# Starting the early units of the maximum pass at slot 15 instead of slot 17 in a two-layer attention kernel

## The reference

```python
x = x + tanh(g_xattn[0]) * xattn0(layernorm(x), ctx, ctx)   # 16 heads of 8, softmax over 154 keys
x = x + tanh(g_ffn[0])   * ffn0(layernorm(x))               # 4-bit weights, 16-bit quantized activations
x = x + tanh(g_xattn[1]) * xattn1(layernorm(x), ctx, ctx)   # the same with a causal mask
x = x + tanh(g_ffn[1])   * ffn1(layernorm(x))               # a gated scan over the batches
```

## Time and profile before

| | |
|---|---|
| device time, median of 3 runs | 343.34 us (343.32 to 343.42) |
| profiled execution, first to last instruction (span) | 341.2 us |
| what lies around the span (median less span) | 2.1 us |
| busy PE, PEld | 279.0 us (82%), 160.7 us (47%) |
| busy DVE, ACT, POOL | 252.5 us (74%), 192.6 us (56%), 136.7 us (40%) |
| reductions of the maximum pass, L1333 | 168, 96.0 us busy |
| exponentials, L772 | 148 in the page's largest group, 82.3 us busy |
| mean granted PE clock | 0.957 |

### The profile page before, as it was taken

One profiled execution on the slowest core, in us unless ns is written; L12 is line 12 of the kernel. 1 busy time (PEld: TensorE's weight loads), 2 busy tenths in 40 slices (PEclk: granted clock), 3 DMA queues, 4 the chain that ended last, 5 costly groups with the idle time before them and its releaser, 6 DMA issues. The chain is left out here.

```text
span 341.2 us, 4468 instructions
## 1 busy us (share of the span) xinstructions
PE 279.0 (82%) x1424; PEld 160.7 (47%) x1424; DVE 252.5 (74%) x538; ACT 192.6 (56%) x303; POOL 136.7 (40%) x274
## 2 busy tenths in 40 slices
PE   0889899899989779985007888899998998999994
PEld 0558544455434345331005776664654654444462
DVE  5699875877996388889989977986596693441834
ACT  1673367556476746779589632446656446665232
POOL 6669893750050411870002059921386207131100
PEclk9999999999999999997556999999999999999998
DMA  7930100010000000000000002220001000000004
GB/s 204 336 146 3 69 32 10 27 73 10 1 8 3 0 0 2 1 0 0 1 0 0 2 0 92 94 100 2 10 25 76 8 0 10 1 0 3 0 1 123
DMA packets 9687, 12.55 MB, mean 37 GB/s; under 512 B 896, under 2 KB 5376, under 8 KB 9664
## 3 DMA queue, kind: packets, MB, share of 16 engines
q1 hardware_dynamic: 9232, 11.80, 9.7%
q10 hardware_dynamic: 432, 0.47, 0.7%
HBM read 4.27 MB, written 1.05 MB: 16 GB/s over the span
## 5 line engine op out<-in xcount | busy, mean ns | idle before, releaser
L1333 DVE TENSOR_REDUCE sb_nm<-ps_top 128x3 f32<-128x462 f32 (+2 forms) x168 | 96.0, 626 | 26.6 <-PE ps_top L953 13.9
L772 ACT ACTIVATE sb_pr<-ps_score 128x512 f32<-128x512 f32 (+1 forms) x148 | 82.3, 583 | 58.8 <-PE ps_score L985 49.2
L953 PE MATMUL ps_top<-sb_Kd,sb_Q 128*128 128x462 f32 (+3 forms) x240 | 69.7, 349 | 4.7 <-DVE sb_nm L1333 2.4
L985 PE MATMUL ps_score<-sb_Q,sb_Kd 128*128 128x512 f32 x119 | 54.4, 467 | 1.3 <-ACT sb_pr L772 1.0
L953 PEld LDWEIGHTS ps_top<-sb_Kd,sb_Q 128*128 128x128 f32 x240 | 42.6, 188 | 18.1 <-DVE sb_nm L1333 11.9
L626 POOL TENSOR_SCALAR sb_var<-sb_mv 128x4 f32<-128x4 f32 x16 | 4.7, 291 | 83.3 <-DVE sb_mv L1296 82.9
L985 PEld LDWEIGHTS ps_score<-sb_Q,sb_Kd 128*128 128x128 f32 x119 | 22.2, 188 | 31.6 <-ACT sb_pr L772 23.4
L1017 PE MATMUL ps_pv<-sb_pr,sb_V 128*32 128x512 f32 x256 | 34.1, 605 | 0.0
L620 POOL TENSOR_SCALAR_AFFINE_SELECT sb_pr<-sb_pr 128x512 f32<-128x512 f32 x16 | 10.6, 661 | 46.4 <-ACT sb_pr L772 46.4
L1353 DVE STREAM_TRANSPOSE sb_oq<-ps_pv 128x512 f32<-128x512 f32 x16 | 10.8, 700 | 12.4 <-PE ps_pv L1017 12.3
L643 POOL TENSOR_SCALAR sb_xn<-sb_xr,sb_nmean,sb_rstd 128x128 f32<-128x128 f32 x44 | 19.3, 453 | 1.2
(11 more groups left out here) (180 smaller groups left out, 556.5 us busy)
## 6 DMA issues: line engine op xcount, KB each, us to landing
sb_Q<-sb_qh SPq DMA_DIRECT2D x16, 256.0 KB, 2.3
sb_Q<-sb_ql SPq DMA_DIRECT2D x8, 256.0 KB, 3.3
sb_xr<-x SPq DMA_DIRECT2D x4, 256.0 KB, 7.7
out<-sb_xr SPq DMA_DIRECT2D x4, 256.0 KB, 2.5
sb_wsb<-w SPq DMA_DIRECT2D x1, 704.0 KB, 9.0
sb_wf<-wffn SPq DMA_DIRECT2D x1, 576.0 KB, 8.6
sb_wkr<-wkr SPq DMA_DIRECT2D x2, 256.0 KB, 7.1
sb_Q<-sb_nmT SPq DMA_DIRECT2D x16, 32.0 KB
```

Source lines behind the costliest of these rows:

```text
L772: act.activation(pr[:, k % PRING, q0:T], score_bank(B * layer + b, t)[:, q0:T], ACT.Exp, scale=SCALE).then_inc(exp_r, 1)
L953: ins = pe.matmul(cols[:, c0:c1, :], Q4[n % 3][:, g, P * qt:P * qt + P], Kd[n % 3][:, g, j:j + c1 - c0, 0:keys], start=True, stop=not mask ...
L985: ins = pe.matmul(ps[:, :], Kd[n % 3][:, g, j, 0:P], Q4[n % 3][:, g, :], start=True, stop=True, skip_group_check=True)
L1333: dve.tensor_reduce(nm[:, :, :].rearrange("p t h -> p (t h)")[:, f0:f0 + heads], top[k % MRING][:, 0:keys * heads].rearrange("p (h k) -> p ...
```

## The change

One constant changes: the early units are spread over the last five slots (15 to 19) instead of the last three (17 to 19), and with `n * EARLY // (EARLY + LAST)` there are two more of them for the batches 2 and 3 of a layer.

```diff
-EARLY, LAST = 3, 13
+EARLY, LAST = 5, 13
```

## The result

The changed kernel takes 338.64 us (median of 6 runs, 338.38 to 340.65) against 343.41 us (6 runs, 343.32 to 344.42): ratio 0.9874, 95% interval [0.9855, 0.9894]. The span of the profiled execution went from 341.2 to 336.7 us, 4.5 us less; the forecast said 3.45 less and 339.9 us.

A forecast was written before the change was run, and what follows sets the result against it. DVE, 93 to 98% busy, was taken to bound the fronts but not the tails. Fronts gain 3.8 us, less 0.35 in the tails, is 3.45: 339.9 us against 343.34, range 338.5 to 342.4.

The forecast's parts named there:

- the price of the fronts: Four fronts: 1.1 us gained in (0,2) and in (1,2), 0.75 in (0,1), 0.85 in (1,1); together 3.8 us.
- its lower end: Range's fast end, 338.5 us: all eight reductions and the narrow units count.
- The 0.2 us of (0,1): Front of (0,1): PE has one unit less before the residual, 0.23 us, so the residual follows by about 0.2.
- The price of 0.54 us for a reduction: DVE: four reductions in a row take 2.27 us and three 1.73, so one more costs 0.54 us.
- POOL would swallow the first one in (0,1): Front of (0,1): the reduction ahead of the division is lost, since POOL holds PE's transposes and DVE only waits longer.
- The tails: Four tails, two more PE units each: +0.35 us taken, because the waits are of the size of the units.
- +0.1 and +0.15: Layer 1 tails: two wide units, 1.1 us, against a 0.73 us wait in (1,1); some returns at slot 19.
- The forecast's own lower bound, -0.3: Tails: -0.3 us if the narrow units at slot 19 pay more than the rest costs.
- PE as the bound of the fronts: Rival: fronts gain only PE's 0.46 us each; 1.5 us in all, 341.8 us; chance 0.21.
- the sign that the forecast had named: Fronts: PE's waits for reductions would be smaller if the forecast was right.
- No change: Rival: only each front's second reduction counts (2.2 us), tails hide nothing (2.5 us); +0.3, 343.6 us; chance 0.08.
- slower: Rival: PE's fixed order grows tails by 2.5 us, fronts give 0.2 each; +1.7, 345.0 us; chance 0.09.

The follow-up runs named there:

- The repeats: Changed kernel with DVE reducing units of the four fronts a second time: two per front 341.09 us; one per front, behind DVE's wait for PE, 339.95 us.
- The early start alone: Kernel before, with early units spread over slots 15 to 19 but batches 2 and 3 keeping their old number, 4 and 3: 342.01 us, ratio 0.9954.
- PE's work put back: Changed kernel with PE computing two units of each of the four fronts twice, DVE's work not put back: 339.86 us.
- the number alone: Kernel before, with 6 and 5 early units for batches 2 and 3, all still in slots 17 to 19: 342.24 us, ratio 0.9982.
- the shift: Changed kernel with units of (0,1) and (1,1) moved to slots ahead of the transposes where PE waits for POOL: 338.33 us, ratio 0.9856 to before.
- both halves put back: Changed kernel with PE computing and DVE reducing two units of each of the four fronts twice: 342.15 us.
- DVE's half alone: Changed kernel with DVE reducing two units of each of the four fronts a second time, into a spare tile; PE's work not put back: 341.09 us.

## Why the prediction was right

The measured 338.64 us lies 1.3 us below the forecast and 0.14 us above the lower end of its range; by the spans 4.5 us were gained where 3.45 had been forecast. The mechanism, DVE's work carried out of full fronts into tails with room, held, and so did the price of the fronts. What the forecast had wrong lies beside it, in the tails and the split. That the range still held is in part luck: its lower end stood for fronts that give all eight reductions, and the time came near it by another sum.

**The fronts.** The two reductions of a front can be told apart by the start of the residual, counted from the first exponential. It moved by -0.08, -0.64, -0.26 and -0.70 us in (0,1), (0,2), (1,1) and (1,2): 1.68 together, where 0.2 + 0.54 + 0.3 + 0.54 = 1.58 had been forecast. The 0.2 us of (0,1) went astray: the unit that left PE's list ahead of the projection to queries only made PE's wait for ACT's copy of the transposed rows longer, before and then after:

```profile
64.53 1.10 PE L936 MATMUL ps_misc<-sb_xnT,sb_wsb 128*128 128x512 f32 x2 [0.36 <-ACT sb_xnT L744]
...
64.45 1.10 PE L936 MATMUL ps_misc<-sb_xnT,sb_wsb 128*128 128x512 f32 x2 [0.58 <-ACT sb_xnT L744]
```

From the residual to the split each front lost 0.55 to 0.56: 2.21, forecast 2.16. The price of 0.54 us for a reduction, and that POOL would swallow the first one in (0,1) and most of it in (1,1), held to within 0.16 us in each front. That the price is DVE's was argued from the waits. The repeats show it for the reduction ahead of the division in (0,2) and (1,2) and for the one behind the statistics in (0,1) and (0,2): 0.53 to 0.55 us each where it is put back behind DVE's last wait, near nothing ahead of it. For the one behind the residual in layer 1 it is read from the traces alone, in which DVE goes from the residual to the split with 0.07 us of idle time in all, before and after.

**The tails** are the step whose size was wrong: +0.35 was forecast, -0.18 measured. In layer 1 the forecast took +0.1 and +0.15 and got -0.12 twice. PE's idle time of 0.72 and 0.79 us fell by 0.72 and 0.73, while its busy time grew by only 0.60 and 0.61 for the two units, because a narrow one now stands in slot 19. The early start alone, with wide units only, shows the first of the two: tails 0.38 us shorter. The forecast's own lower bound, -0.3, had this mechanism in it; the value taken had the wrong sign. (A slip without weight: 1.62 of 6.38 us is 25%, not 26.)

**The split** is the term that was missing, 0.44 us in (0,1) and (0,2). The forecast counted only instructions that move. These two did not move in the order; they moved in time, away from POOL's instructions.

**The rivals.** PE as the bound of the fronts: four fronts gave 3.9 us, not 1.8, and DVE's idle time in them did not grow by what was taken away, but for (1,1), from 0.33 to 0.90 us. PE's weight loads waited 1.6, 2.6, 0.6 and 1.3 us for reductions in the four fronts before and 0.5, 1.7, 0.2 and 1.0 after, the sign that the forecast had named. But the rival had something: of the 1.8 us that PE's work put back would have cost by it, 0.9 came, all ahead of the division. No change and slower fell with the tails; the number alone shows that the half of slower that lies in the tails is true without the early start: 3.0 us in the tails, more than the 2.5 of that rival. No first unit waits for a DMA.

## What to carry over

Where an engine fills one stretch and idles in the next, price the moved work at both ends: its spacing in a full queue where it leaves, and where it lands the wait that stands ahead of it in the other engine's list. Work put ahead of a wait that is long enough was free here; behind the engine's last wait it cost all of its length, unless another engine's wait further on took it, as POOL's did in (0,1) and (1,1). The same two units in each tail made 3.2 us of difference in the tails by their place alone. And when a stretch moves in time, look at what then stands beside its short critical instructions on the other engines, here POOL.

## What the runs showed of the hardware

A cast and a subtraction of 64 columns take 0.22 and 0.27 us in the split of (1,0), with nothing on POOL beside them. Beside POOL's instructions on SBUF the subtraction took up to 0.41 us, and the cast up to 0.69: that is the first split of layer 1, which the change does not touch. In every trace here its cast takes 0.53 to 0.69 us and ends about 0.07 us behind POOL's subtraction for the queries' low part (`ql`, L614); in the changed kernel:

```profile
218.70 0.69 DVE L1344 CAST sb_nms<-sb_nm 128x64 fp32r<-128x64 f32 x1
```

```profile
218.06 1.26 POOL L614 TENSOR_TENSOR sb_ql<-sb_qf,sb_qh 128x512 fp32r<-128x512 f32 x1
```

In single executions a stretch of a few microseconds ran for the most part at the lower level of TensorE's clock, 1.2 GHz (means of 0.57 to 0.69 in windows around it), and cost a microsecond or more. Windows of the shift in the front of (0,0), which took 11.15 us in that execution and 10.15 in the others, then of the kernel with both halves put back, in (0,1), whose front took 19.00 us and with DVE's half alone 17.39:

```profile
40.10:44.00 3.90, 3.90 (x15) 3.28 (x13) 3.33 (x7) 2.87 (x5) 3.21 (x9) 0.57 0.14 54
44.00:46.00 2.00, 2.00 (x15) 0.91 (x14) 2.00 (x4) 1.70 (x4) 1.83 (x4) 1.00 0.34 131
```

```profile
64.00:66.00 2.00, 1.63 (x3) 0.75 (x3) 1.97 (x4) 0.71 (x2) 1.00 (x2) 0.62 0.00 0
```

In the second PE had waited 1.12 us for POOL and 0.58 for ACT just before; in the first only 0.26 for DVE. In the changed kernel waits of 1.37 and 0.58 us stand at the place of the second, and the clock there is 1.00. What sets it off was not tried.
